# Second attention with its scores laid out by keys: TensorE alternates score chunks of the tile two ahead with value products of the present one

## The chip, the cores and the metric

One core of a Trainium2 chip runs the whole program. The metric is the device time of one execution in microseconds (us). Engines: PE is TensorE (PEld its weight loads), DVE VectorE, ACT ScalarE, POOL GpSimd, SP SyncE, which here only starts transfers. They run their own instruction lists and meet at semaphores.

## What is computed

The program runs a convolutional attention block on 4 images of 48x48 tokens with 128 channels, then full self-attention over the 2304 tokens of each image, then a routed expert layer. Only the second attention (`layer1_attention`) is touched:

```
def _L1_attn_ref(x, Wq, bq, Wk, bk, Wv, bv):
    q = x @ Wq + bq
    k = x @ Wk + bk
    v = x @ Wv + bv
    scores = jnp.einsum('btd,bsd->bts', q, k)
    attn = jax.nn.softmax(scores, axis=-1)
    return jnp.einsum('bts,bsd->btd', attn, v)

t = t + _L1_attn_ref(_ln_t(t), ...)     # t: 4 images x 2304 tokens x 128
```

Everything is float32. One attention head has 128 channels, so for each image the score matrix is 2304x2304.

## The kernel before

An image has 18 query tiles (`TILES`) of 128 tokens. Keys come in 6 chunks (`NG`) of 384, that is 3 blocks of 128 (`GB`). `lnT` holds the normalised tokens with channels on partitions; the key weights are folded into the queries, so `lnT` serves as the keys and `qT` as the queries. `v` holds the values by tokens, and in one more column a per-token constant that is added to the scores.

For each query tile the engines do this, with 128 queries on partitions:

- PE (`scores`, L1264): six products of 128x384 into `Sps`, with the query tile as the stationary weights; VectorE (`stage`, L1456) copies that tile out of `qT` first.
- DVE (`take_scores`, L1463): adds the constant, writes the chunk to `S` and keeps its row maximum; L1467 makes the negative maximum of the six.
- ACT (`tile`, L1140): one exponential over 128x2304, whose bias is that maximum, with the row's total as a by-product.
- PE (`attend`, L1287): 18 transposes of the exponentials into `Tps`, since the value product needs keys on partitions. ACT (L1148) copies them to `PT` in six pieces of 128x384.
- PE (`values`, L1278): 18 products of 128x128, with a block of `PT` as the stationary weights, added up in `Ops`.
- DVE (`take_row`, L1471 and L1477; `row_statistics`, L1483 to L1489): scales by the inverse total, adds to the token rows, and takes their mean and variance.

PE works one tile ahead with the scores. All instructions stand in hand-written order, one list for each engine. Into the tiles of images 0 to 2 the preparation of the next image is spread (`PROJECT` at tile 8, `TRANSPOSE` at 11, `TO_Q` at 12, `TO_V` at 14 on PE; sums, statistics and normalisation on DVE behind tiles 0, 1, 3, 5, 6, 8, 9 and 10). In the last image the results are normalised by POOL (`normal`, L1088) and transposed by PE ahead of tiles 5, 8 and 11 for the expert layer. POOL otherwise adds a bias to the next image (`bias`, L1075, 128x384 x6) and computes `rstd2`.

Of the kernel before, what the change touches and what calls it, by code (L numbers as in the profile page):

```python
# [20 lines left out]
P = 128  # L21
# [911 lines left out]
def layer1_attention(nc, a, s, ident, conv_bias, x1, ln2, ln2T, sums, first_num, first_in, first_den, den_in):  # L933
# [4 lines left out]
    with ExitStack() as ctx:  # L938
# [10 lines left out]
        PT = ln2T[:, 3, :].rearrange("p (t q) -> p t q", t=TILES)  # L949
# [4 lines left out]
        v = sb("v", [P, 2 * TILES, C + 1])  # L954
# [4 lines left out]
        q_tile = sb("q_tile", [P, 2, P])  # L959
        S = sb("S", [P, 2, N])  # L960
        weights = sb("weights", [P, 3, C])
# [12 lines left out]
        part_max = sb("part_max", [P, 2, NG])  # L974
        neg_max = sb("neg_max", [P, 2])
        total = sb("total", [P, 2])
# [7 lines left out]
        Sps = ps("Sps", [P, 3, BANK])  # L984
        Tps = ps("Tps", [P, 3, BANK])
# [13 lines left out]
        q_staged, s_ready, s_taken = sem("q_staged"), sem("s_ready"), sem("s_taken")  # L999
        max_ready, p_ready, inv_step, row_step = sem("max_ready"), sem("p_ready"), sem("inv_step"), sem("row_step")  # L1000
        moments_ready, rstd_step, rstd_ready, ln2_ready = sem("moments_ready"), sem("rstd_step"), sem("rstd_ready"), sem("ln2_ready")

        S_SLOTS = T_SLOTS = 3
        O_SLOTS = 2
        S_USES = NG * TILES
# [8 lines left out]
        def t_at(b, qt, last=False, after=True):  # L1014

            if last:
                return T_PREP + (T_PREP + NG * TILES) * b + NG * (qt + sum(qt >= x if after else qt > x for x in TO_EXPERTS))
            prep = sum(qt >= x if after else qt > x for x in (TRANSPOSE, TO_Q))
            return T_PREP + (T_PREP + NG * TILES) * b + NG * (qt + prep)

        def o_at(b, qt, last=False, after=True):
            prep = 0 if last else sum(qt >= x if after else qt > x for x in (PROJECT, TO_V))
            return O_PREP + (O_PREP + TILES) * b + qt + NG * prep
# [37 lines left out]
        def _(pool):  # L1061
# [41 lines left out]

        @block.scalar
        def _(act):
            for i, w in enumerate(("Wo0", "Wq1", "Wk1")):
                act.dma_start(weights[:, i, :], a[w]).then_inc(weights_in, 16)
            act.dma_start(value[:, 0:C], a["Wv1"]).then_inc(weights_in, 16)
# [7 lines left out]
            def take_transposes(n, i, groups=range(NG)):  # L1116
                for g in groups:
                    act.wait_ge(t_ready, n + g + 1)
                    act.activation(lnT[:, bass.ds((i % 2) * N + g * GW, GW)], Tps[:, g % T_SLOTS, 0:GW], ACT.Copy).then_inc(t_taken, 1)

            def take_queries(n, i):
                for g in range(NG):
                    act.wait_ge(t_ready, n + g + 1)
                    alone(act)
                    act.activation(qT[:, bass.ds((i % 2) * N + g * GW, GW)], Tps[:, g % T_SLOTS, 0:GW], ACT.Identity,
                                   bias=query[:, C:C + 1]).then_inc(t_taken, 1)

            def take_normal(b, n, groups):
                for g in groups:
                    act.wait_ge(t_ready, n + g + 1)  # L1130
                    act.activation(ln2T[:, b, cols(GW, g)], Tps[:, g % T_SLOTS, 0:GW], ACT.Copy,
                                   accum_out=sums[:, b, g:g + 1]).then_inc(t_taken, 1)

            BEFORE, BEHIND = range(T_SLOTS), range(T_SLOTS, NG)

            def tile(b, qt, t, last=False, before=None, prepare=()):
                if before is not None:
                    before()
                act.wait_ge(max_ready, TILES * b + qt + 1)
                act.activation(S[:, t, :], S[:, t, :], ACT.Exp, bias=neg_max[:, t:t + 1],  # L1140
                               accum_out=total[:, t:t + 1]).then_inc(p_ready, 1)
                for step in prepare:
                    step()
                for g in range(NG):
                    if g == 0:
                        act.wait_ge(o_ready, o_at(b, qt, last))
                    act.wait_ge(t_ready, t_at(b, qt, last) + g + 1)
                    act.activation(PT[:, cols(GB, g), :], Tps[:, g % T_SLOTS, 0:GW].rearrange("p (t q) -> p t q", t=GB),  # L1148
                                   ACT.Copy).then_inc(t_taken, 1)
# [20 lines left out]
            for b in range(B - 1):  # L1170
                prepare = {
                    TRANSPOSE - 1: [lambda: deviations(b + 1)],
# [837 lines left out]
```

## Time and profile before

| | us |
|---|---|
| median of 3 runs (lowest, highest) | 3510.87 (3508.09, 3511.03) |
| profiled execution, its own time | 3511.96 |
| its span | 3510.2 |
| tiles of the second attention, first score product to last row | 2575.4 to 3347.9 |
| expert layer's first instruction on PE | 3353.66 |

Busy over the span: PE 3403.2 us (97%), PEld 2643.6, DVE 2635.0, ACT 2015.6, POOL 1645.1. In the profile a PE instruction's time reaches to its modelled end, and neighbours overlap; the distance between starts is what the engine spends.

### The profile page before, as it was taken

The numbers are of one execution on the slowest core, as the hardware profiler recorded it, in microseconds if no ns is written. First come the engines' busy times: TensorE is split into PE (matmuls) and PEld (weight loads), VectorE is DVE, ScalarE is ACT, GpSimd is POOL, SyncE is SP. The second block draws the span as 40 slices with busy tenths as digits, with TensorE's granted clock in tenths as the row PEclk, the third lists the DMA queues.
The fourth block names the chain that finished last, engine by engine and source line by source line (L and its number), as shares of the span: only waits on it lengthen the run. The fifth ranks groups of instructions, "written<-read, shape, count | busy, mean of one in ns | idle before, by whom it ended". The sixth has DMA issues, their size and how long they took to land. (4 is left out here: it accounts for less than half of the span.)

```text
span 3510.2 us, 94134 instructions
## 1 busy us (share of the span) xinstructions
PE 3403.2 (97%) x30646; PEld 2643.6 (75%) x30646; DVE 2635.0 (75%) x6494; ACT 2015.6 (57%) x3642; POOL 1645.1 (47%) x863
## 2 busy tenths in 40 slices
PE   8799999999999999999999999999799999999978
PEld 5477777777777777777777777777578888888867
DVE  8688888888888888888888888888666675654457
ACT  4466666666666666666666666666435454455533
POOL 5566656556556556656656655655400001005112
PEclk9899999999999999999999999999899999999989
DMA  7642242234224224222422422222331020100011
GB/s 266 194 133 94 72 135 94 72 106 123 73 99 129 72 92 136 73 92 100 109 92 94 115 92 94 81 91 94 106 99 58 15 85 4 39 1 1 1 44 42
DMA packets 111794, 308.21 MB, mean 88 GB/s; under 512 B 11592, under 2 KB 72955, under 8 KB 91163
## 3 DMA queue, kind: packets, MB, share of 16 engines
q1 hardware_dynamic: 110629, 306.27, 27.9%
q8 instruction: 68, 1.11, 0.1%
q10 hardware_dynamic: 1054, 0.48, 0.1%
q14 instruction: 43, 0.35, 0.0%
HBM read 252.38 MB, written 54.31 MB: 87 GB/s over the span
## 5 line engine op out<-in xcount | busy, mean ns | idle before, releaser
L730 ACT ACTIVATE c_PT<-c_Tps 128x512 f32<-128x512 f32 x2592 | 1428.3, 604 | 877.8 <-PE c_Tps L860 815.7
L795 DVE CUSTOM_DVE_ANT_0 c_S<-c_Sps,mask_tiles 128x768 f32<-128x768 f32 x1728 | 1619.3, 956 | 412.6 <-PE c_Sps L849 371.8
L698 POOL TENSOR_SCALAR c_S<-c_S,c_row_max 128x2304 f32<-128x2304 f32 x576 | 1414.0, 2455 | 950.6 <-DVE c_row_max L806 950.6
L860 PE MATMUL c_Tps<-ident,c_S 128*128 128x128 f32 x10368 | 1400.8, 273 | 4.1 <-ACT c_PT L730 4.1
L860 PEld LDWEIGHTS c_Tps<-ident,c_S 128*128 128x128 f32 x10368 | 1229.7, 140 | 152.1 <-ACT c_PT L730 9.7
L849 PE MATMUL c_Sps<-c_K,c_Q 96*128 (+1 forms) x3456 | 854.6, 328 | 29.0 <-DVE c_part_max L795 14.6
L873 PE MATMUL c_Ops<-c_PT,c_V 128*32 128x256 f32 x10368 | 619.2, 382 | 0.8 <-ACT c_PT L730 0.8
L873 PEld LDWEIGHTS c_Ops<-c_PT,c_V 128*32 128x32 f32 x10368 | 307.4, 109 | 243.6 <-issue 51.1
L849 PEld LDWEIGHTS c_Sps<-c_K,c_Q 96*128 96x128 bf16 x3456 | 315.2, 98 | 188.4 <-issue 144.1
L1463 DVE TENSOR_SCALAR_CACHE_REDUCE l_S<-l_Sps,l_v 128x384 f32<-128x384 f32 x432 | 259.8, 618 | 252.9 <-PE l_Sps L1264 249.3
L1148 ACT ACTIVATE ln2T<-l_Tps 128x384 f32<-128x384 f32 x432 | 196.5, 491 | 363.6 <-PE l_Tps L1287 363.6
L1278 PE MATMUL l_Ops<-l_v,ln2T 128*128 128x128 f32 x2592 | 336.3, 275 | 0.1
L1278 PEld LDWEIGHTS l_Ops<-l_v,ln2T 128*128 128x128 f32 x2592 | 317.6, 192 | 19.1 <-issue 0.6
L1080 POOL TENSOR_SCALAR l_rstd<-l_moments 128x3 f32<-128x3 f32 x24 | 5.6, 235 | 681.0 <-DVE l_moments L1489 681.0
L788 DVE SCALAR_TENSOR_TENSOR c_conv<-c_vpad,taps,c_conv (+1 forms) x216 | 304.9, 1412 | 10.4 <-issue 5.6
L1264 PE MATMUL l_Sps<-l_lnT,l_q_tile 128*128 128x384 f32 x864 | 305.8, 488 | 2.2 <-issue 0.9
L1264 PEld LDWEIGHTS l_Sps<-l_lnT,l_q_tile 128*128 128x128 f32 x864 | 151.9, 190 | 85.0 <-DVE l_S L1463 13.8
L1287 PE MATMUL l_Tps<-ident,l_S 128*128 128x128 f32 x1296 | 188.9, 273 | 1.5 <-ACT l_S L1140 0.8
L1287 PEld LDWEIGHTS l_Tps<-ident,l_S 128*128 128x128 f32 x1296 | 152.8, 141 | 25.4 <-issue 12.2
L1140 ACT ACTIVATE l_S<-l_S,l_neg_max 128x2304 f32<-128x2304 f32 x72 | 159.0, 2208 | 8.6 <-DVE l_neg_max L1467 8.6
L795 DVE DVE_READ_ACCUMULATOR2_ANT c_part_max<- 128x1 f32 x1728 | 143.5, 83 | 0.0
L1693 ACT ACTIVATE e_hid<-e_Hps,e_b 128x384 f32<-128x384 f32 x96 | 55.7, 582 | 65.2 <-PE e_Hps L1728 62.2
(223 smaller groups left out, 1644.2 us busy)
## 6 DMA issues: line engine op xcount, KB each, us to landing
mask_tiles<-in_mask SPq DMA_DIRECT2D x144, 1152.0 KB, 7.7
numerators<-c_O SPq DMA_DIRECT2D x288, 64.0 KB
mask_tiles<-numerators SPq DMA_DIRECT2D x7, 2304.0 KB, 8.5
q_parts<-c_PT SPq DMA_DIRECT2D x12, 576.0 KB, 4.4
k_parts<-c_PT SPq DMA_DIRECT2D x12, 576.0 KB
c_Q<-q_parts SPq DMA_DIRECT2D x71, 96.0 KB
c_vpad<-v_padded SPq DMA_DIRECT2D x8, 756.0 KB, 14.8
c_K<-k_parts SPq DMA_DIRECT2D x7, 864.0 KB, 8.6
```

The costliest lines, as they stand in the source:

```text
L698: pool.tensor_scalar(S[:, slot, :], S[:, slot, :], -1.0, row_max[:, slot:slot + 1], ALU.mult, ALU.add).then_inc(shifted, 1)
L730: act.activation(dst, src, ACT.Exp, scale=-1.0).then_inc(exp_done, 1)
L788: dve.scalar_tensor_tensor(out=dst, in0=window[:, :, 0:W], scalar=taps[:, bass.ds(tap, 1)], in1=dst, op0=ALU.mult, op1=ALU.add).then_inc(c ...
L795: dve.tensor_tensor_reduce(out=S[:, r % ROW_SLOTS, cols(CH, c)].rearrange("p (k n) -> p k n", k=2), in0=Sps[:, n % S_SLOTS, :, 0:GW], in1= ...
L849: last = pe.matmul(Sps[:, n % S_SLOTS, k, 0:GW], Q[:, p, r // 2, cols(P, r % 2)], K[:, bass.ds(start, GW)], start=True, stop=True)
L860: last = pe.transpose(Tps[:, g % T_SLOTS, cols(P, k)], S[:, (2 * b + t) % ROW_SLOTS, cols(P, kt)], ident[:, :])
L873: last = pe.matmul(Ops[32 * j:32 * (j + 1), image, :], V[:, b * TILES + kt, :], PT[:, image, kt, :], start=kt < COLS, stop=kt >= TILES - COLS)
L1148: act.activation(PT[:, cols(GB, g), :], Tps[:, g % T_SLOTS, 0:GW].rearrange("p (t q) -> p t q", t=GB), ACT.Copy).then_inc(t_taken, 1)
L1264: pe.matmul(Sps[:, g % S_SLOTS, 0:GW], q_tile[:, t, :], lnT[:, bass.ds((b % 2) * N + g * GW, GW)], start=True, stop=True).then_inc(s_ready, 1)
L1278: product = pe.matmul(Ops[:, t, 0:C], PT[:, kt, :], v[:, (b % 2) * TILES + kt, 0:C], start=kt == 0, stop=kt == TILES - 1)
L1287: block_t = pe.transpose(Tps[:, g % T_SLOTS, cols(P, k)], S[:, t, cols(P, g * GB + k)], ident[:, :])
L1463: dve.tensor_scalar(S[:, t, cols(GW, g)], Sps[:, g % S_SLOTS, 0:GW], v[:, (b % 2) * TILES + qt, C:C + 1], None, ALU.add, ALU.max, accum_ou ...
```

## The change

Scores are computed with keys on partitions: `lnT`'s block of 128 keys is the stationary operand and the query tile (read straight from `qT`, so `stage` is gone) streams through it, 18 products of 128x128 in six chunks. The exponentials then stand as the value product needs them, and the 18 transposes of a tile and their copies go. What goes with them:

- ACT copies each score chunk from `Tps` (now four slots) to one of three buffers `keys_by` (`take_scores`).
- The maximum of a query now lies across partitions and blocks. DVE reduces the nine blocks of each half (`half_maximum`: 128x1152 in, 128x128 out, read with the block index innermost, so each element lies 128 words behind the last), joins the halves (`key_maximum`), PE turns that 128x128 tile (`turn_max`), DVE reduces it to one number per query and writes it into a 128x128 tile together with the constant (`query_maximum`), PE turns that back (`spread_max`), and ACT copies it to `shift` (`take_shift`).
- `shift` is subtracted from all 18 blocks: the first nine by DVE, the last nine by POOL (`subtract_max`, 128x1152 each). ACT then takes the exponential of each half (`exponentials`).
- `v` gets a column of ones, so the value product of 129 columns also gives the total; `take_row` inverts it.
- PE alternates: chunk g of tile j+2, then the three value products g of tile j, six times; `turn_max(j+1)` stands after g=1 and `spread_max(j+1)` after g=2.
- POOL's bias, deviations and normalisations are spread over the tiles behind its subtraction.

The core of the diff (functions rewritten in full are shown as after):

```diff
-        Sps = ps("Sps", [P, 3, BANK])
-        Tps = ps("Tps", [P, 3, BANK])
+        Tps = ps("Tps", [P, 4, BANK])
+        Mps = ps("Mps", [P, 2, BANK])
+        P_SLOTS = 3
+        keys_by = [slot.rearrange("p (t q) -> p t q", t=TILES) for slot in (S[:, 0, :], S[:, 1, :], ln2T[:, 3, :])]
...
@@ gpsimd
+            def subtract_max(j):
+                pool.wait_ge(shift_in, j + 1)
+                part = keys_by[j % P_SLOTS][:, HALVES[1].start:HALVES[1].stop, :]
+                pool.tensor_tensor(part, part, shift[:, :, :].to_broadcast([P, len(HALVES[1]), P]), ALU.subtract).then_inc(shifted_pool, 1)
...
@@ scalar
+            for j in range(1, ALL):
...
+                if j + AHEAD < ALL:
+                    take_scores(j + AHEAD, range(TURN + 2))
+                if j + 1 < ALL:
+                    take_shift(j + 1)
+                if j + AHEAD < ALL:
+                    take_scores(j + AHEAD, range(TURN + 2, NG - 1))
+                if j + 1 < ALL:
+                    exponentials(j + 1, 0)
+                if j + AHEAD < ALL:
+                    take_scores(j + AHEAD, range(NG - 1, NG))
+                if j + 1 < ALL:
+                    exponentials(j + 1, 1)
...
@@ tensor
+                for g in range(NG):
+                    if j + AHEAD < ALL:
+                        scores(j + AHEAD, range(g, g + 1))
+                    values(j, g)
+                    if j + 1 < ALL and g == TURN:
+                        turn_max(j + 1)
+                    if j + 1 < ALL and g == TURN + 1:
+                        spread_max(j + 1)
...
@@ vector
+            def half_maximum(j, half):
+                dve.wait_ge(t_taken, scores_at(j) + NG * (half + 1) // 2 + T_SLOTS)
+                part = keys_by[j % P_SLOTS][:, HALVES[half].start:HALVES[half].stop, :].rearrange("p t q -> p q t")
+                dve.tensor_reduce(half_max[:, half, :], part, AX.X, ALU.max).then_inc(half_step, 1)
...
+            def query_maximum(j):
+                dve.wait_ge(turned_max, j + 1)
+                dve.tensor_reduce(query_max[:, :], Mps[:, 0, 0:P], AX.X, ALU.max).then_inc(query_step, 1)
...
+                dve.scalar_tensor_tensor(out=max_wide[:, :], in0=query_max[:, :].to_broadcast([P, P]), scalar=constant,
+                                         in1=constant.to_broadcast([P, P]), op0=ALU.add, op1=ALU.subtract).then_inc(wide_max, 1)
...
+            def subtract_max(j):
+                dve.wait_ge(shift_in, j + 1)
...
+            for j in range(ALL):
+                if j:
+                    take_row(j - 1)
...
+                if j:
+                    row_statistics(j - 1)
+                if j and j + 1 < ALL:
+                    query_maximum(j + 1)
+                if j + AHEAD < ALL:
+                    half_maximum(j + AHEAD, 0)
+                if j + 1 < ALL:
+                    subtract_max(j + 1)
+                if j + AHEAD < ALL:
+                    half_maximum(j + AHEAD, 1)
+                    key_maximum(j + AHEAD)
```

How it moves instructions. On PE, one tile in the middle of an image, before (x is the number of products; the 6 score products stand as 5 and 1):

```order
L1264 MATMUL l_Sps<-l_lnT,l_q_tile 128x384 x5
L1287 MATMUL l_Tps<-ident,l_S 128x128 x9
L1264 MATMUL l_Sps<-l_lnT,l_q_tile 128x384
L1278 MATMUL l_Ops<-l_v,ln2T 128x128 x3
L1287 MATMUL l_Tps<-ident,l_S 128x128 x3
L1278 MATMUL l_Ops<-l_v,ln2T 128x128 x3
L1287 MATMUL l_Tps<-ident,l_S 128x128 x3
L1278 MATMUL l_Ops<-l_v,ln2T 128x128 x3
L1287 MATMUL l_Tps<-ident,l_S 128x128 x3
L1278 MATMUL l_Ops<-l_v,ln2T 128x128 x9
```

and the first three and a half of the six rounds of such a tile after:

```order
L1310 MATMUL l_Tps<-l_qT,l_lnT 128x128 x3
L1330 MATMUL l_Ops<-l_v,l_S 128x129 x3
L1310 MATMUL l_Tps<-l_qT,l_lnT 128x128 x3
L1330 MATMUL l_Ops<-l_v,l_S 128x129 x3
L1316 MATMUL l_Mps<-ident,l_key_max 128x128
L1310 MATMUL l_Tps<-l_qT,l_lnT 128x128 x3
L1330 MATMUL l_Ops<-l_v,l_S 128x129 x3
L1322 MATMUL l_Mps<-ident,l_max_wide 128x128
L1310 MATMUL l_Tps<-l_qT,l_lnT 128x128 x3
```

The transposes of whole score tiles have left PE, and two single ones that carry the maximum stand between the rounds.

On DVE, the same place before:

```order
L1463 TENSOR_SCALAR l_S,l_part_max<-l_Sps,l_v 128x384 x6
L1467 TENSOR_REDUCE l_neg_max<-l_part_max 128x1
L1456 COPY l_q_tile<-l_qT 128x128
L1471 RECIPROCAL l_inv_total<-l_total 128x1
L1477 SCALAR_TENSOR_TENSOR x<-l_Ops,l_inv_total,x 128x128
L1483 BN_STATS l_row_stats<-x 128x6
L1486 BN_AGGR l_row_moments<-l_row_stats 128x2
L1489 COPY l_moments<-l_row_moments 128x2
```

and after:

```order
L1527 RECIPROCAL l_inv_total<-l_Ops 128x1
L1529 SCALAR_TENSOR_TENSOR x<-l_Ops,l_inv_total,x 128x128
L1536 BN_STATS l_row_stats<-x 128x6
L1539 BN_AGGR l_row_moments<-l_row_stats 128x2
L1542 COPY l_moments<-l_row_moments 128x2
L1509 TENSOR_REDUCE l_query_max<-l_Mps 128x1
L1516 SCALAR_TENSOR_TENSOR l_max_wide<-l_query_max,l_v 128x128
L1500 TENSOR_REDUCE l_half_max<-l_S 128x128
L1522 TENSOR_TENSOR l_S<-l_S,l_shift 128x1152
L1500 TENSOR_REDUCE l_half_max<-l_S 128x128
L1504 TENSOR_TENSOR l_key_max<-l_half_max 128x128
```

The six reads of PSUM have become two reductions and a subtraction over half a tile each, and four of the eleven rows now belong to tiles one or two ahead.

## Rows read from the trace of the kernel before

**Rows 1.** Page, part 5: busy us, mean ns | idle before, TensorE and ScalarE groups of this stage.

```profile
L1278 PE MATMUL l_Ops<-l_v,ln2T 128*128 128x128 f32 x2592 | 336.3, 275 | 0.1
...
L1264 PE MATMUL l_Sps<-l_lnT,l_q_tile 128*128 128x384 f32 x864 | 305.8, 488 | 2.2 <-issue 0.9
...
L1287 PE MATMUL l_Tps<-ident,l_S 128*128 128x128 f32 x1296 | 188.9, 273 | 1.5 <-ACT l_S L1140 0.8
...
L1148 ACT ACTIVATE ln2T<-l_Tps 128x384 f32<-128x384 f32 x432 | 196.5, 491 | 363.6 <-PE l_Tps L1287 363.6
```

**Rows 2.** Windows: length, busy PE, PEld, DVE, ACT, POOL, granted clock, DMA share, GB/s.

```profile
2619.45:2814.51 195.06, 194.44 (x1291) 160.31 (x1290) 121.13 (x423) 97.49 (x160) 12.48 (x18) 1.00 0.14 45
...
2764.34:2774.19 9.85, 9.85 (x68) 8.21 (x67) 4.94 (x19) 4.92 (x9) 0.00 (x0) 1.00 0.00 0
...
2555.00:2565.00 10.00, 6.08 (x20) 3.85 (x21) 6.44 (x30) 3.26 (x7) 0.00 (x0) 0.63 1.03 398
```

**Rows 3.** Timeline, TensorE, one tile: start us, us, engine, line.

```profile
2762.43 2.17 PE L1278 MATMUL l_Ops<-l_v,ln2T 128*128 128x128 f32 x18
...
2764.44 3.39 PE L1264 MATMUL l_Sps<-l_lnT,l_q_tile 128*128 128x384 f32 x10
...
2767.67 1.15 PE L1287 MATMUL l_Tps<-ident,l_S 128*128 128x128 f32 x9
...
2774.30 0.49 PE L1264 MATMUL l_Sps<-l_lnT,l_q_tile 128*128 128x384 f32 x1
```

**Rows 4.** Timeline, VectorE, the same tile and the next.

```profile
2765.39 0.62 DVE L1463 TENSOR_SCALAR_CACHE_REDUCE l_S<-l_Sps,l_v 128x384 f32<-128x384 f32 x1 [3.50 <-PE l_Sps L1264]
...
2770.37 0.16 DVE L1471 RECIPROCAL l_inv_total<-l_total 128x1 f32<-128x1 f32 x1
...
2770.45 0.33 DVE L1477 SCALAR_TENSOR_TENSOR x<-l_Ops,l_inv_total,x 128x128 f32<-128x128 f32 x1
...
2774.56 0.35 DVE L1477 SCALAR_TENSOR_TENSOR x<-l_Ops,l_inv_total,x 128x128 f32<-128x128 f32 x1 [2.82 <-PE l_Ops L1278]
...
2775.82 0.62 DVE L1463 TENSOR_SCALAR_CACHE_REDUCE l_S<-l_Sps,l_v 128x384 f32<-128x384 f32 x1
```

**Rows 5.** Groups by form over the whole run, VectorE: busy us, mean ns.

```profile
L1354 DVE TENSOR_TENSOR mask_tiles<-mask_tiles 128x1152 f32<-128x1152 f32 x12 | 15.6, 1344 | 0.0
...
L1841 DVE TENSOR_TENSOR mask_tiles<-mask_tiles,e_b2s 128x2304 f32<-128x2304 f32 x4 | 10.2, 2551 | 0.0
...
L1796 DVE TENSOR_REDUCE e_r<-e_greater 4x8 f32<-4x128 f32 x1 | 0.3, 274 | 0.0
...
L1506 DVE COPY l_bo_all<-l_Tps 128x128 f32<-128x128 f32 x3 | 0.7, 281 | 0.0
...
L1870 DVE SCALAR_TENSOR_TENSOR mask_tiles<-mask_tiles,e_ymv,e_gamma 128x128 f32<-128x128 f32 x72 | 20.6, 341 | 0.0
...
L1347 DVE TENSOR_TENSOR l_den_sum<-first_den 128x144 f32<-128x144 f32 x4 | 1.2, 307 | 0.1
```

**Rows 6.** Groups by form over the whole run, GpSimd.

```profile
L271 POOL TENSOR_TENSOR f_rot_sum<-f_rot_sum,c_PT 128x768 f32<-128x768 f32 x23 | 38.2, 1659 | 42.0 <-ACT c_PT L315 41.9
...
L1075 POOL TENSOR_TENSOR ln2T<-ln2T,l_bo_all 128x384 f32<-128x384 f32 x24 | 23.2, 1000 | 28.1 <-DMA ln2T<-in_x 28.1
```

**Rows 7.** Timeline, GpSimd and VectorE at 2777 us, and VectorE at 2525 us.

```profile
2777.10 5.84 POOL L1075 TENSOR_TENSOR ln2T<-ln2T,l_bo_all 128x384 f32<-128x384 f32 x6
...
2781.05 2.07 DVE L1344 TENSOR_TENSOR first_den<-first_den 128x144 f32<-128x144 f32 x2
...
2525.49 0.53 DVE L1344 TENSOR_TENSOR first_den<-first_den 128x144 f32<-128x144 f32 x2 [0.57 <-DMA first_den<-denominators]
```

**Rows 8.** Groups by form, ScalarE.

```profile
L1140 ACT ACTIVATE l_S<-l_S,l_neg_max 128x2304 f32<-128x2304 f32 x72 | 159.0, 2208 | 8.6 <-DVE l_neg_max L1467 8.6
...
L1160 ACT ACTIVATE l_query<-l_Ops 128x129 f32<-128x129 f32 x1 | 0.3, 280 | 2.0 <-PE l_Ops L1207 2.0
```

**Rows 9.** Timeline, ScalarE, inside the tile of rows 3.

```profile
2768.26 1.26 ACT L1148 ACTIVATE ln2T<-l_Tps 128x384 f32<-128x384 f32 x3 [2.94 <-PE l_Tps L1287]
```

More of the change, by code:

```diff
@@ L1130, in take_normal @@
                     act.wait_ge(t_ready, n + g + 1)
-                    act.activation(ln2T[:, b, cols(GW, g)], Tps[:, g % T_SLOTS, 0:GW], ACT.Copy,
+                    act.activation(ln2T[:, b, cols(GW, g)], Tps[:, (n + g) % T_SLOTS, 0:GW], ACT.Copy,
                                    accum_out=sums[:, b, g:g + 1]).then_inc(t_taken, 1)
[L1134 to L1149, printed above, removed]
@@ L1180, in normal_part @@
[L1180 to L1187 removed]
+            take_scores(0, range(NG))
+            take_scores(1, range(NG))
@@ new lines, in _ @@
+            take_shift(0)
+            take_scores(2, range(4))
+            exponentials(0, 0)
+            take_scores(2, range(4, NG))
+            exponentials(0, 1)
+            take_shift(1)
+            for half in range(2):
+                exponentials(1, half)
+            for j in range(1, ALL):
+                b, qt = j // TILES, j % TILES
+                if b == B - 1:
+                    if qt in TO_EXPERTS:
+                        take_normal(TO_EXPERTS.index(qt), t_at(j))
+                elif qt == TRANSPOSE:
+                    take_transposes(t_at(j), b + 1)
+                elif qt == TO_Q:
+                    take_queries(t_at(j), b + 1)
+                if j + AHEAD < ALL:
[10 more added lines that the diff above has]
+                    exponentials(j + 1, 1)
+                if b + 1 < B and qt == TRANSPOSE - 1:
+                    deviations(b + 1)
@@ L1324, in _ @@
-            for qt in range(TILES):
-                if qt in TO_EXPERTS:
-                    transpose_normal(TO_EXPERTS.index(qt), t_at(B - 1, qt, last=True, after=False))
-                following = (B - 1, qt + 1, (qt + 1) % 2) if qt + 1 < TILES else None
-                if following is not None:
-                    scores(*following, groups=FIRST)
-                attend(B - 1, qt, qt % 2, last=True, last_scores=following)
+            scores(0, range(NG))
+            scores(1, range(3))
@@ new lines, in _ @@
+            turn_max(0)
+            scores(1, range(3, NG))
+            spread_max(0)
+            scores(2, range(4))
+            turn_max(1)
+            scores(2, range(4, NG))
+            pe.wait_ge(o_taken, O_PREP + O_SLOTS)
+            for g in range(NG):
+                values(0, g)
+                if g == 2:
+                    spread_max(1)
+            for j in range(1, ALL):
+                b, qt = j // TILES, j % TILES
+                if b == B - 1:
+                    if qt in TO_EXPERTS:
+                        transpose_normal(TO_EXPERTS.index(qt), t_at(j))
+                elif qt == PROJECT:
+                    project(b + 1, o_at(j, after=False))
+                elif qt == TRANSPOSE:
+                    transpose_ln(b + 1, t_at(j))
+                elif qt == TO_Q:
+                    to_q(b + 1, t_at(j))
+                elif qt == TO_V:
+                    to_v(b + 1, o_at(j, after=False))
+                for g in range(NG):
+                    if j + AHEAD < ALL:
[5 more added lines that the diff above has]
+                        spread_max(j + 1)
```

373 lines of the change are left out of this document (167 added, 206 removed).

## The prediction

> **What bounds the kernel now.** I read the page's groups of the stage first, then windows, then one tile on each engine. The stage takes 772.5 us of the span (the tiles run from 2575.4 to 3347.9). In a window that spans one whole image TensorE is busy for 194.44 of 195.06 us, and in one of a single plain tile for 9.85 of 9.85, at full clock, while VectorE and ScalarE are busy for about half of it [rows 2]. So a tile costs what TensorE needs, and the timeline takes that apart [rows 3]. 18 instructions of value products last 2.17 us together and one of them 0.275 [rows 1], so they start (2.17 - 0.275)/17 = 0.1115 us apart; each float32 product is two instructions, so 0.223 us. Transposes: (1.15 - 0.273)/8 = 0.110. Score instructions of 384 columns: (3.39 - 0.488)/9 = 0.322. A tile is 12 x 0.322 + 18 x 0.110 + 36 x 0.1115 = 3.87 + 1.98 + 4.01 = 9.86 us, and its starts are 2774.30 - 2764.44 = 9.86 apart. VectorE waits for TensorE at the tile's head (3.50 us idle [rows 4]).
>
> **What the change does to TensorE.** 18 score products of 128 columns with new weights each are what the value products already are: 0.223 each, 4.01 us, against 3.87. The transposes go (-1.98), two single ones come (+0.22), and one column more in 36 instructions adds 36 x 0.1115/128 = 0.03. TensorE's tile is 3.87 -> 4.01, in sum 8.28 us, 1.58 less. If TensorE stayed the bound, 72 tiles would give back 114 us.
>
> **What it does to the others.** I follow the order of each list around one tile, since VectorE now stands between every two steps. A hop from one engine to another I take as 0.1 us: the third transpose of rows 3 ends at 2767.67 + 2 x 0.110 + 0.273 = 2768.16, and ScalarE's copy starts at 2768.26 [rows 9]. Starting from the moment at which `query_maximum` can run:
>
> 1. `query_maximum`: a reduction of 128 numbers from PSUM, 0.28 (the 4x128 reduction took 0.274, a PSUM copy of 128 0.281 [rows 5]), 0.1 for the own semaphore, and a 128x128 SCALAR_TENSOR_TENSOR, 0.34 [rows 5]: 0.72.
> 2. hop, `spread_max` 0.28, hop, `take_shift` 0.28 (128x129 from PSUM [rows 8]), hop: 0.86. Meanwhile VectorE does `half_maximum(j+2, 0)`, so it is not waiting when `shift` arrives, and POOL is.
> 3. POOL's subtraction over 128x1152. 384 elements took 1.000 and 768 took 1.659 us [rows 6]; another 384 make 1.659 + 0.659 = 2.32.
> 4. VectorE's subtraction, also with both operands in SBUF. Such an instruction does not run beside POOL's: two 128x144 ones took 0.53 us alone and 2.07 while POOL worked through its six of 128x384, which start 0.97 apart [rows 7], so each waited for one POOL instruction to end. I take it that it starts after POOL's: 1.3 (1152 elements are 1.344 alone [rows 5]).
> 5. hop, then ScalarE's `exponentials(j+1, 0)`. From 129 to 384 columns a ScalarE instruction grows by 0.211 us [rows 1, 8], 0.83 ns a column; 2304 take 2.208, so 1152 take 2.208 - 0.953 = 1.25. Only behind it stands the copy of the sixth score chunk, 0.385 (three take 1.26, the last 0.49 [rows 9]). Hop. In all 1.84, in which VectorE has nothing, because its next instruction needs that chunk.
> 6. `half_maximum(j+2, 1)`, h, then `key_maximum`, 0.33 with its own semaphore (0.307 for 144 elements [rows 5]).
> 7. `take_row` and `row_statistics` of the finished tile. From the reciprocal to the scaling 0.08, from the scaling to the first instruction behind the statistics 1.26 [rows 4]: 1.34. Then step 1 again.
>
> The circle is 0.72 + 0.86 + 2.32 + 1.3 + 1.84 + h + 0.33 + 1.34 = 8.71 + h. `turn_max` is in time in a plain tile: TensorE starts the next tile's values 1.35 us after step 4 ends, needs 0.67 + 1.34 us to reach it, and VectorE gets there after 1.84 + h + 0.33.
>
> h is a reduction over 1152 elements each 512 bytes from the last, and no row has such a read. Contiguous, 128 elements take 0.274 and 1152 of another instruction 1.344; were each element to cost two, it would be the 2.551 of 2304 elements [rows 5]. Between 1.34 and 2.55 neither end is nearer in kind; I take the middle, 1.95. The circle is 10.66, rounded to 10.6 for what the 0.1 hops overstate: 0.75 more than 9.85.
>
> The Trainium skill (Vector Engine (DVE) Microarchitecture Reference, section 5.2, on the access granule) has a table for element orders: 1.054 ns a column contiguous, 1.73 when a source hops on every element, and 2.50 at a step of 24 words. That would be an estimate of 1152 x 1.73 + 80 = 2.07 us, or 2.96, and the circle by it 10.7 or 11.6. The trace here can't show it.
>
> **Preparation.** It was hidden under TensorE and is no longer. VectorE is busy 121.13 us in an image's window and 4.94 in a plain tile [rows 2], so 121.13 - 18 x 4.94 = 32.2 us an image are preparation. 12 instructions of 0.56 of it (PSUM to `x` and to `v`, 6.7 us) run against TensorE's 18 products of 0.223. Those two tiles then need another round and a half before `turn_max`: 4.0 + 2.7 - 1.3 is about 5.5 each instead. The other 25.5 us stand in series in the circle. At `TRANSPOSE` and `TO_Q` ScalarE's six copies begin only behind both exponentials, and `turn_max` comes about 2.3 us late, twice. Together 25.5 + 11 + 4.6 = 41 us an image. Before, an image took 195.06 - 18 x 9.85 = 17.8 us above its tiles. So three images get 18 x 0.75 + 23 = 36.7 us longer, 110; the last one 13.5 and 1 for the transposes of the expert layer; the first tile starts its values later, but no scores are left at the end: 0. In all +124 us. The profiled execution took 3511.96, 1.1 above the median of the runs: 3511.96 + 124 = 3636.
>
> **Rivals.**
> - *The read costs nothing extra.* h = 1.34, 0.61 less in 72 circles: -44, so 3592. For it: VectorE's rows are all alike per element. Against: all of them read neighbours.
> - *The read costs two elements or more.* h = 2.55: +43, 3679. The page named above has a step at which it is dearer still, and its 2.96 as an estimate would give 3709.
> - *Faster: the two subtractions run side by side.* If VectorE's does not wait for POOL's, it starts when `half_maximum(j+2, 0)` ends, and the circle is 0.72 + h + 1.34 + 1.84 + h + 0.33 + 1.34 = 5.57 + 2h. With h = 1.34 that is 8.25, and TensorE's 8.28 decide: 1.57 less a tile, -113, against 3 x 20 for preparation (23 less a little that VectorE's spare time takes up) and 1: about 3460. It ends below the kernel before only up to a circle of 8.9 (72 x 0.95 are those 69), h about 1.65; with h = 1.95 (9.47) it gives 3554. For it: only one place in the stage shows POOL in VectorE's way, and in 128x144. Against: that place is clear, 2.07 against 0.53.
> - *The clock.* TensorE waits 2.3 of 10.6 us. At 61% busy the granted clock was 0.63 [rows 2], a mixture of its two levels (1.2 and 2.4 GHz). At the lower one a tile would be 16.6 us and the time about 4000. It would stay busy then, so at worst this comes in pieces; it decides only where a stretch falls below a clock of 8.28/10.6 = 0.78.
>
> **How the numbers follow.** Forecast case (POOL first, h from 1.6 to 2.3, 3611 to 3662): 0.58. Costlier read: 0.15. Free read with the wait for POOL: 0.10. Side by side with a costly read: 0.05. Side by side with a free one, faster: 0.08. Clock: 0.04. A price of POOL of 3 x 0.97 instead of 2.32 adds 43 us, and hops of 0.05 take off 14. The range, 3570 to 3720, leaves out the faster case, the side-by-side ones and the clock. Runs of the kernel before differ by 0.08%; within 0.2% (7 us) I call the same. Faster 0.08, same 0.02, slower 0.90.
>
> **What would show it.** TensorE's tile without waits at 8.3 us but starts 10.6 apart, with idle time before `spread_max`, `turn_max` and a tile's first value product; L1500 at 1.95 us; VectorE's L1522 long, from the end of L1500 to 1.3 us behind POOL's L1096, which takes 2.3; 1.8 us of idle VectorE before each second L1500; an image 232 us long. Wrong would be L1522 at 1.34 beside a running L1096, or TensorE without waits.

## The result, and the profile after

| | before | after |
|---|---|---|
| median, us (lowest, highest) | 3509.70 (3508.09, 3511.03), 4 runs | 3667.28 (3666.41, 3670.36), 4 runs |
| profiled execution, span | 3511.96, 3510.2 | 3667.56, 3665.8 |
| mean granted clock over the span | 0.985 | 0.971 |
| expert layer's first instruction on PE | 3353.69 | 3510.37 |

The ratio is 1.045, 95% interval 1.0436 to 1.0464: 157 us slower. All of it arises in this stage, since the expert layer starts 156.7 us later. (The 3353.66 of the table before the prediction is the start of that instruction's weight load.) The groups of the stage, of TensorE, VectorE, GpSimd and ScalarE, in place of those of [rows 1] (busy us, mean ns | idle before):

```profile
L1310 PE MATMUL l_Tps<-l_qT,l_lnT 128*128 128x128 f32 x2592 | 375.5, 284 | 0.0
...
L1096 POOL TENSOR_TENSOR l_S<-l_S,l_shift 128x1152 f32<-128x1152 f32 x48 | 128.8, 2683 | 443.1 <-ACT l_shift L1170 443.1
...
L1330 PE MATMUL l_Ops<-l_v,l_S 128*128 128x129 f32 x1728 | 254.5, 286 | 31.4 <-ACT l_S L1175 31.4
L1500 DVE TENSOR_REDUCE l_half_max<-l_S 128x128 f32<-128x1152 f32 x96 | 208.2, 2169 | 82.6 <-ACT l_S L1165 82.6
...
L1175 ACT ACTIVATE l_S<-l_S 128x1152 f32<-128x1152 f32 x96 | 111.2, 1158 | 65.8 <-DVE l_S L1522 64.3
```

TensorE's value products now stand idle before them (31.4 us, for the exponentials), where L1278 had 0.1 [rows 1]. Windows of one image, of one plain tile, and of two stretches in the tile of `TO_V`, to be read beside [rows 2] (length, busy PE, PEld, DVE, ACT, POOL, granted clock, DMA share, GB/s):

```profile
2820.46:3062.94 242.48, 190.02 (x1436) 178.38 (x1435) 187.56 (x281) 103.10 (x178) 70.76 (x36) 0.92 0.11 37
2809.72:2820.46 10.74, 8.95 (x76) 8.41 (x75) 8.72 (x12) 5.16 (x10) 4.82 (x3) 1.00 0.00 2
2779.00:2784.00 5.00, 5.00 (x24) 5.00 (x25) 1.95 (x4) 0.00 (x0) 0.00 (x0) 0.50 0.00 0
2784.00:2789.00 5.00, 5.00 (x45) 5.00 (x45) 2.32 (x7) 1.43 (x3) 0.00 (x0) 0.97 0.01 3
```

The roles are exchanged. An image takes 242.48 us instead of 195.06, and a plain tile 10.74 instead of 9.85. TensorE was busy for all of that tile and is for 8.95 us of it now (its modelled ends included), at full clock; VectorE went from 4.94 to 8.72, and of the 2.02 us left 1.61 are one wait. One turn of the circle in the timeline of VectorE, with GpSimd's and ScalarE's parts under it (start us, us, engine, line, [idle before it <- what ended that]):

```profile
2765.15 2.18 DVE L1500 TENSOR_REDUCE l_half_max<-ln2T 128x128 f32<-128x1152 f32 x1 [1.61 <-ACT ln2T L1165]
2767.37 0.29 DVE L1504 TENSOR_TENSOR l_key_max<-l_half_max 128x128 f32<-128x128 f32 x1
2767.58 0.16 DVE L1527 RECIPROCAL l_inv_total<-l_Ops 128x1 f32<-128x1 f32 x1
...
2768.98 0.28 DVE L1509 TENSOR_REDUCE l_query_max<-l_Mps 128x1 f32<-128x128 f32 x1
2769.30 0.35 DVE L1516 SCALAR_TENSOR_TENSOR l_max_wide<-l_query_max,l_v 128x128 f32<-128x128 f32 x1
2769.57 2.17 DVE L1500 TENSOR_REDUCE l_half_max<-l_S 128x128 f32<-128x1152 f32 x1
2771.67 2.62 DVE L1522 TENSOR_TENSOR ln2T<-ln2T,l_shift 128x1152 f32<-128x1152 f32 x1
2775.89 2.11 DVE L1500 TENSOR_REDUCE l_half_max<-l_S 128x128 f32<-128x1152 f32 x1 [1.61 <-ACT l_S L1165]
...
2770.43 2.64 POOL L1096 TENSOR_TENSOR ln2T<-ln2T,l_shift 128x1152 f32<-128x1152 f32 x1 [8.10 <-ACT l_shift L1170]
...
2774.32 1.16 ACT L1175 ACTIVATE ln2T<-ln2T 128x1152 f32<-128x1152 f32 x1 [1.74 <-DVE ln2T L1522]
2775.39 0.47 ACT L1165 ACTIVATE l_S<-l_Tps 128x384 f32<-128x384 f32 x1
2775.76 1.15 ACT L1175 ACTIVATE ln2T<-ln2T 128x1152 f32<-128x1152 f32 x1
```

From the second half's reduction to the next such one it is 2775.89 - 2765.15 = 10.74 us. VectorE's subtraction (L1522) is on record as 2.62 us, because it starts at 2771.67 beside GpSimd's, which ends at 2773.07, and ends 1.22 behind it. Then VectorE stands idle for 1.61 us, until ScalarE has done an exponential half and, behind it, the copy of the sixth score chunk. Every step of the circle is in these rows.

### The profile page after: what moved, and what is told of

It reads as the page before. It is cut to its first block and busy times, and to the rows that moved or that the text cites. A ratio compares the mean times of both kernels' runs of the same rounds, so it can differ in the third digit from the quotient of the medians.

```text
span 3665.8 us, 94647 instructions
## 1 busy us (share of the span) xinstructions
PE 3367.5 (92%) x31222; PEld 2699.3 (74%) x31222; DVE 2903.7 (79%) x5918; ACT 2035.4 (56%) x3714; POOL 1881.2 (51%) x936
## 5 line engine op out<-in xcount | busy, mean ns | idle before, releaser
L1310 PE MATMUL l_Tps<-l_qT,l_lnT 128*128 128x128 f32 x2592 | 375.5, 284 | 0.0
L1096 POOL TENSOR_TENSOR l_S<-l_S,l_shift 128x1152 f32<-128x1152 f32 x48 | 128.8, 2683 | 443.1 <-ACT l_shift L1170 443.1
L1310 PEld LDWEIGHTS l_Tps<-l_qT,l_lnT 128*128 128x128 f32 x2592 | 347.3, 203 | 1.1
L1330 PE MATMUL l_Ops<-l_v,l_S 128*128 128x129 f32 x1728 | 254.5, 286 | 31.4 <-ACT l_S L1175 31.4
L1500 DVE TENSOR_REDUCE l_half_max<-l_S 128x128 f32<-128x1152 f32 x96 | 208.2, 2169 | 82.6 <-ACT l_S L1165 82.6
L1165 ACT ACTIVATE l_S<-l_Tps 128x384 f32<-128x384 f32 x288 | 138.9, 487 | 210.8 <-PE l_Tps L1310 210.7
L1330 PEld LDWEIGHTS l_Ops<-l_v,l_S 128*128 128x128 f32 x1728 | 228.0, 201 | 37.0 <-issue 37.0
L1096 POOL TENSOR_TENSOR ln2T<-ln2T,l_shift 128x1152 f32<-128x1152 f32 x24 | 64.4, 2683 | 183.0 <-ACT l_shift L1170 183.0
L1175 ACT ACTIVATE l_S<-l_S 128x1152 f32<-128x1152 f32 x96 | 111.2, 1158 | 65.8 <-DVE l_S L1522 64.3
L1500 DVE TENSOR_REDUCE l_half_max<-ln2T 128x128 f32<-128x1152 f32 x48 | 104.5, 2177 | 38.8 <-ACT ln2T L1165 38.8
L1330 PE MATMUL l_Ops<-l_v,ln2T 128*128 128x129 f32 x864 | 122.9, 280 | 5.6 <-ACT ln2T L1175 5.5
```

The costliest lines, as they stand in the source:

```text
L1096: pool.tensor_tensor(part, part, shift[:, :, :].to_broadcast([P, len(HALVES[1]), P]), ALU.subtract).then_inc(shifted_pool, 1)
L1165: act.activation(keys_by[j % P_SLOTS][:, cols(GB, g), :], Tps[:, (scores_at(j) + g) % T_SLOTS, 0:GW].rearrange("p (t q) -> p t q", t=GB), ...
L1310: last = pe.matmul(Tps[:, (n + g) % T_SLOTS, cols(P, k)], lnT[:, bass.ds((b % 2) * N + (g * GB + k) * P, P)], query_tile, start=True, stop ...
L1330: last = pe.matmul(Ops[:, qt % 2, 0:C + 1], keys_by[j % P_SLOTS][:, kt, :], v[:, (b % 2) * TILES + kt, 1:C + 2], start=kt == 0, stop=kt == ...
L1500: dve.tensor_reduce(half_max[:, half, :], part, AX.X, ALU.max).then_inc(half_step, 1)
```

## The experiments

Two edits act on links of the circle (e2, e3), one on the reduction (e1), and one on where the preparation stands (e4). The others put these together and follow what then decides. "Plain tile" is a tile without preparation, as the distance between the starts of `query_maximum`; "image" is the third one, between the same starts (the second differs from it by up to 1.7 us); "preparation" is an image less 18 plain tiles. The row "before" has the second image, between first score products. Each ratio is against executions of the kernel before from the same round, whose medians lie between 3509.1 and 3509.7.

| kernel | time, us (lowest, highest) | ratio, 95% interval | plain tile | image | preparation |
|---|---|---|---|---|---|
| before | 3509.70 | 1 | 9.85 | 195.06 | 17.8 |
| after | 3667.28 | 1.045 (1.0436 to 1.0464) | 10.74 | 242.4 | 49.1 |
| e1 contiguous reductions | 3615.10 (3614.10, 3617.04) | 1.0303 (1.0286 to 1.0320) | 9.90 | 229.0 | 50.8 |
| e2 sixth copy first | 3573.47 (3572.69, 3577.66) | 1.0187 (1.0170 to 1.0204) | 9.40 | 218.4 | 49.2 |
| e3 shift from PSUM | 3589.01 (3588.28, 3590.64) | 1.0228 (1.0211 to 1.0245) | 9.46 | 225.3 | 55.0 |
| e4 preparation in the gap | 3649.77 (3648.93, 3652.17) | 1.0403 (1.0386 to 1.0420) | 10.74 | 235.2 | 41.9 |
| e5 = e2 + e3 | 3557.46 (3554.25, 3558.36) | 1.0134 (1.0118 to 1.0149) | 8.88 | 215.1 | 55.3 |
| e6 = e5 + e4 | 3525.02 (3523.41, 3527.34) | 1.0043 (1.0027 to 1.0058) | 8.88 | 204.6 | 44.8 |
| e7 = e5 + contiguous | 3513.64 (3511.32, 3517.26) | 1.0012 (1.0002 to 1.0021) | 8.88 | 201.4 | 41.6 |
| e8 = e5 + sums on GpSimd | 3534.54 (3533.45, 3535.24) | 1.0072 (1.0058 to 1.0085) | 8.88 | 208.2 | 48.4 |
| e9 = e5 + scores earlier | 3505.94 (3504.91, 3510.80) | 0.9994 (0.9985 to 1.0003) | 8.38 | 201.4 | 50.6 |
| e10 = e6 + sums + scores earlier | 3489.24 (3484.12, 3490.05) | 0.9939 (0.9925 to 0.9952) | 8.37 | 194.8 | 44.1 |
| e11 = e7 + scores earlier | 3471.07 (3469.69, 3472.84) | 0.9889 (0.9874 to 0.9904) | 8.26 | 191.2 | 42.5 |

**e1: what the reduction's read costs.** In `half_maximum`:

```diff
-                part = keys_by[...][:, HALVES[half].start:HALVES[half].stop, :].rearrange("p t q -> p q t")
+                part = keys_by[...][:, HALVES[half].start:HALVES[half].stop, :].rearrange("p t q -> p (t q)").rearrange("p (q t) -> p q t", t=TILES // 2)
```

> The two reductions of a half tile read the same 1152 numbers in the order in which they lie, so what they give is no maximum per query; all else as in the changed kernel (3667). My theory: the circle through VectorE sets each tile (10.74 us), the second reduction of each tile lies on it and the first is hidden behind GpSimd's subtraction. The reduction goes from 2.17 to 1.34 us, the circle to 9.9, the time falls by 72 x 0.83 = 60 to about 3607. Rival A, TensorE is what lasts (its granted clock fell to 0.9 in this stage and its products lie further apart): the reductions are beside the point and the time falls by under 10. Rival B, both reductions lie in series: 120 less.

The groups of VectorE:

```profile
L1522 DVE TENSOR_TENSOR l_S<-l_S,l_shift 128x1152 f32<-128x1152 f32 x48 | 157.1, 3273 | 4.2 <-ACT l_shift L1170 4.2
L1500 DVE TENSOR_REDUCE l_half_max<-l_S 128x128 f32<-128x1152 f32 x96 | 129.7, 1351 | 84.2 <-ACT l_S L1165 84.0
```

The same 1152 elements take 1.351 us when neighbours are read, and 2.169 when each lies 512 bytes from the last. Both reductions of a tile got 0.82 shorter, but the tile only by 0.84 in all: the first one ended sooner into the wait for GpSimd, and L1522 grew from 2500 to 3273 ns. So one reduction of the two lies on the circle, as the prediction had it. The run gained 52 us of the 60 expected, since preparation grew by 1.7 us an image. A cheap read alone doesn't make the change pay.

**e2: the idle stretch.** In ScalarE's list:

```diff
-                    take_scores(j + AHEAD, range(TURN + 2, NG - 1))
+                    take_scores(j + AHEAD, range(TURN + 2, NG))
                 if j + 1 < ALL:
                     exponentials(j + 1, 0)
-                if j + AHEAD < ALL:
-                    take_scores(j + AHEAD, range(NG - 1, NG))
-                if j + 1 < ALL:
                     exponentials(j + 1, 1)
```

> ScalarE copies the sixth score chunk ahead of the first exponential, not behind it. My theory: VectorE's 1.61 us of idle time before each second reduction goes, the circle becomes 9.1 to 9.2 (the other circle, through exponential, first value products and turn_max, is 9.0 and lies just below), 110 us less: about 3557. Rival: the exponential comes later, TensorE's first value products wait for it in its place, and the circle through TensorE keeps the time within 20 us of 3667.

```profile
L1497 DVE TENSOR_REDUCE l_half_max<-l_S 128x128 f32<-128x1152 f32 x96 | 208.2, 2170 | 26.5 <-ACT l_S L1165 26.5
```

L1497 is `half_maximum` in this kernel. The idle time ahead of it falls from 82.6 to 26.5 us, the tile by 1.34, and the run by 94 us: of the three costs that were cut one by one (e1 to e3) the largest is the order of two ScalarE instructions. The tile came 0.2 to 0.3 us longer than expected.

**e3: the shared access of VectorE and GpSimd.** VectorE's subtraction reads the shift where TensorE left it, in PSUM, instead of the SBUF copy; GpSimd keeps the copy. `spread_max` then waits for that subtraction instead of the copy.

```diff
-                    pe.wait_ge(shift_in, j)
+                    pe.wait_ge(shifted_dve, j)
...
-                dve.tensor_tensor(part, part, shift[:, :, :].to_broadcast([P, len(HALVES[0]), P]), ALU.subtract)
+                dve.tensor_tensor(part, part, Mps[:, 1:2, 0:P].to_broadcast([P, len(HALVES[0]), P]), ALU.subtract)
```

> VectorE's subtraction reads the shift from PSUM and not from its SBUF copy, so only one of its operands lies in SBUF; it still waits for the copy. My theory: it need no longer wait for GpSimd's subtraction, lasts 1.36 us right behind the first reduction, the circle loses 1.25 us, 90 less: about 3577, and GpSimd's subtraction stays at 2.64. Rival: the instruction lasts 2.6 us for another reason (in place, broadcast operand) and the time does not move; or from PSUM it is slower by itself.

VectorE and GpSimd in a plain tile, where GpSimd's subtraction starts first:

```profile
3207.07 1.34 DVE L1522 TENSOR_TENSOR ln2T<-ln2T,l_Mps 128x1152 f32<-128x1152 f32 x1
...
3205.84 2.64 POOL L1096 TENSOR_TENSOR ln2T<-ln2T,l_shift 128x1152 f32<-128x1152 f32 x1 [7.09 <-ACT l_shift L1170]
```

Side by side and each at its own price, in all 72 tiles (1.335 to 1.359 us and 2.632 to 2.659). The wait was for what two SBUF operands need and not for the data, which are the same. The tile loses 1.28 us, the run 78 and not 90, since preparation grew from 49.1 to 55.0 us an image.

**e4: preparation into the idle stretch.** The steps that stood behind `key_maximum` (`invert`, `sum_half` and so on) stand ahead of it and of the second half's reduction:

```diff
                     subtract_max(j + 1)
+                if b + 1 < B:
+                    if qt == 0:
+                        invert(b + 1)
...
                 if j + AHEAD < ALL:
                     half_maximum(j + AHEAD, 1)
                     key_maximum(j + AHEAD)
```

> The eight pieces of preparation on VectorE stand between its subtraction and the second reduction, where it idles 1.61 us, not behind the reduction. My theory: preparation is in series in the circle, and here each piece hides up to 1.6 us of itself: seven of 1.6 and one of 1.2 in three images, 37 less, some of it lost to GpSimd's bias: 3630 to 3640. Rival: preparation costs by its transfers, TensorE and ScalarE parts, and the time stays within 8 us of 3667.

7.2 us an image came back, of at most 8 x 1.6 = 13 that the idle stretches of the eight tiles with such steps hold. The run gained 17.5 us: between the theory (27 to 37) and the rival (under 8). In the second image the tiles of seven of the steps got 1.0 to 1.8 us shorter, but the tile of `PROJECT` 1.0 longer, and that of `normalise` and `TRANSPOSE` stayed at 19 us. Some steps grew there beside GpSimd's subtraction: `sum_half`'s L1399 took up to 2.04 us, 1.59 on average, instead of 1.36.

**e5: both links.**

> The two edits of the second and third experiment together: the sixth copy ahead of the middle value products, and VectorE's subtraction reading the shift from PSUM. My theory (a circle of 18 x waits between VectorE and GpSimd sets a tile's period): the two act on different links, 1.34 us (10.74 to 9.40) and 1.28 us (10.74 to 9.46) off the circle, so a tile that does nothing else takes 8.1 to 8.4 us, where TensorE's own 8.28 us begins to matter; with the preparation as before the time is 3667 - 94 - 78 = 3495, and less of a gain where TensorE's 8.28 takes over, 3500 to 3515. A rival, that one of the two gains came through the same wait as the other (the idle time ahead of the exponentials), would leave the circle at 9.3 to 9.4 and the time near 3570.

Neither. 8.88 is neither 8.1 to 8.4 nor 9.3, and the run fell 62 us short of the sum of the two gains (3495). Something new decides at 8.88.

**e6, e7, e8: what decides then.**

> The fifth experiment with the preparation steps ahead of the second half's reduction, as in the fourth. If the fourth experiment gained (18 us) because the steps filled VectorE's idle stretch ahead of that reduction, there is next to nothing left to fill once that stretch is gone, and this one ends within 10 us of the fifth. If it gained because the steps in that place stretch less beside GpSimd or reach TensorE sooner, it is again 15 to 20 us under the fifth.

> The fifth experiment with the second half's reduction over neighbouring elements, of the same size: its maximum is no longer the one of each query, so the outputs differ. VectorE's part of a tile falls by another 0.8 us (2.17 to 1.35). If the fifth is held by TensorE's instructions (8.28 us in a tile that does nothing else), such a tile stays at 8.28 to 8.35, and only the tiles with preparation gain, some 5 to 10 x 0.8 us an image, so 12 to 25 us in all. If VectorE's circle still sets the period there, every tile gains up to 0.8 us, some 40 us in all.

> The fifth experiment with the additions of the partial sums, 3.9 us of VectorE in each of two tiles of an image, done by GpSimd in the tiles 1, 2, 5 and 6, where it has 3 to 4 us free beside its two steps. If VectorE's work in those tiles adds to the period as it did in the changed kernel (tiles 3.9 us longer), the time falls by 3 x 2 x 3.9 = 23 us against the fifth, to some 3480 to 3490. If GpSimd's additions (near 2 us each) come in the way of its subtraction, or stretch VectorE beside them, the gain is under 8 us.

In e7 both halves' reductions read neighbours (the expectation names only the second), so VectorE has 0.8 us less to do in each half, and the plain tile stays at 8.88 to the hundredth. The run gained 44 us all the same, near the 40 of the theory that failed, but nearly all of it in preparation (55.3 to 41.6 us an image). So VectorE isn't what holds it there, and 8.88 isn't TensorE's 8.28 either. TensorE's timeline of e7, its first value products in two tiles that follow each other, gives the reason:

```profile
3197.05 0.91 PE L1327 MATMUL l_Ops<-l_v,l_S 128*128 128x129 f32 x6 [0.38 <-ACT l_S L1175]
...
3205.93 0.91 PE L1327 MATMUL l_Ops<-l_v,ln2T 128*128 128x129 f32 x6 [0.38 <-ACT ln2T L1175]
```

TensorE waits in every tile for the first exponential half. The idle time is reckoned from modelled ends; by starts, the score chunk ahead and these value products take 1.96 us together instead of 1.34, and 0.62 on top of the 8.26 that e11 shows is 8.88. By e2's edit that half stands behind the sixth copy, and the copy behind the last score chunk, which TensorE computes only one group of value products before. It is e2's gain on one engine turned into a wait on another, hidden as long as VectorE was later still.

e6 was meant as a control and fell outside both theories: 32 us under e5, where 0 or 15 to 20 were expected. An image lost 10 to 11 us, most of it in two tiles: 3.9 in the one behind `statistics` (12.85 to 8.96 in the second image) and 2.7 in that of the second `finish_half`. The rows of the first are TensorE's. First e5's, in the timeline and in windows:

```profile
2915.23 0.48 PE L1319 MATMUL l_Mps<-ident,l_max_wide 128*128 128x128 f32 x1 [3.19 <-DVE l_max_wide L1513]
2915.50 1.49 PE L1307 MATMUL l_Tps<-l_qT,l_lnT 128*128 128x128 f32 x6
```

```profile
2916.00:2921.00 5.00, 5.00 (x25) 5.00 (x25) 2.50 (x2) 1.00 (x3) 2.64 (x1) 0.50 0.00 0
2921.00:2926.00 5.00, 4.62 (x40) 4.46 (x39) 3.63 (x21) 3.46 (x5) 0.00 (x0) 0.98 0.00 0
```

Then e6's, the same two views:

```profile
2896.15 0.34 PE L1313 MATMUL l_Mps<-ident,l_key_max 128*128 128x128 f32 x1 [1.80 <-DVE l_key_max L1501]
2896.32 0.83 PE L1307 MATMUL l_Tps<-l_qT,l_lnT 128*128 128x128 f32 x6
```

```profile
2895.00:2900.00 5.00, 3.53 (x30) 3.34 (x31) 4.58 (x10) 1.26 (x3) 1.13 (x1) 1.00 0.00 0
```

In e5 the step (`statistics`, 3.57 us) stands between `key_maximum` and the next `query_maximum`, and TensorE stands for 3.19 us before `spread_max`. Then its clock is granted at 0.50, which is 1.2 GHz: in the next 5 us six instructions (three products) take 1.29 us instead of 0.67. In e6 the same step delays `turn_max` instead, TensorE stands for 1.80 us, and the clock stays at 1.00. From 2820 to 3020 us the mean clock is 0.93 in e5 and 0.97 in e6, and TensorE's idle time before `spread_max` 16.2 and 1.7 us (before `turn_max` in e6 8.0). So the placing is worth more than the idle stretch it fills, and part of it may be the clock. How much of the 32 us is clock and how much the shorter wait wasn't tried by itself.

e8 moves the additions to GpSimd:

```diff
+            def sum_pairs(i, half):
+                pool.wait_ge(half_in, 16 * (2 * i + half - 1))
+                for x in (0, 2):
+                    last = pool.tensor_tensor(num[:, x, :], num[:, x, :], num[:, x + 1, :], ALU.add)
+                last.then_inc(sum_step, 1)
...
+                if b + 1 < B and qt in (1, 2):
+                    (sum_pairs if qt == 1 else sum_sums)(b + 1, 0)
+                if b + 1 < B and qt in (5, 6):
+                    (sum_pairs if qt == 5 else sum_sums)(b + 1, 1)
```

The time fell by 23 us, as expected (from 3557 that is 3534; the 3480 to 3490 of the expectation doesn't follow from its own sum), but otherwise than expected: an addition takes GpSimd 2.65 us, where I had put 2, and because the second `finish_half` went one tile later, the tile of `PROJECT` took 20.2 us instead of 16.7.

**e9: the new wait.** In TensorE's list the sixth score chunk goes ahead of the fifth group of value products:

```diff
                 for g in range(NG):
-                    if j + AHEAD < ALL:
-                        scores(j + AHEAD, range(g, g + 1))
+                    if j + AHEAD < ALL and g < NG - 1:
+                        scores(j + AHEAD, range(g, NG if g == NG - 2 else g + 1))
                     values(j, g)
```

> The fifth experiment, with the sixth score chunk of the tile two ahead computed before the fifth group of value products instead of after it. In the fifth and the seventh experiment alike a plain tile took 8.88 us, in each TensorE stood 0.4 to 0.5 us before its first value products (for ScalarE's first exponential half, which stands behind the sixth copy). My theory now: 8.28 us of instructions and this wait make the 8.88. Then the sixth copy comes 0.67 us sooner, the wait goes, and a plain tile takes 8.3 to 8.5 us (VectorE's own circle with the strided reduction is near 8.45): 0.4 us x some 45 tiles, 3535 to 3542 us. If instead VectorE's circle holds the 8.88 (the seventh showed that it doesn't alone), the time stays at 3557.

The group of value products of e5, and then of e9:

```profile
L1327 PE MATMUL l_Ops<-l_v,l_S 128*128 128x129 f32 x1728 | 252.6, 285 | 17.5 <-ACT l_S L1175 17.5
```

```profile
L1327 PE MATMUL l_Ops<-l_v,l_S 128*128 128x129 f32 x1728 | 239.5, 280 | 0.9 <-ACT l_S L1175 0.9
```

The wait is gone and the plain tile is 8.38, in the expected range. The run gained 51 us, more than twice the 15 to 22 expected: all 72 tiles got 0.5 us shorter and not some 45 (36 us), and the preparation 4.7 us an image (14), which I hadn't counted. This kernel can't be told from the one before.

**e10 and e11.**

> The sixth experiment (both edits, preparation ahead of the second half's reduction), with the edit of the ninth, and with the additions of the partial sums done by GpSimd (the first half's in the tiles 1 and 2, the second's in 4 and 5, so that the steps that use them stay where they are in the sixth). By the parts: 3525 - 17 for the wait - 19 for the additions (tiles of 11.6, 9.9 and 12.7 us in the sixth, of 11.4, 9.1 and 10.3 in the eighth) = 3489, between 3480 and 3500, which is under the kernel before (3509). If GpSimd's additions come in the way of its subtraction as they did in the tile after the eighth's sixth, 3500 to 3510.

> The seventh experiment (second half's maxima not taken per query) with the edit of the ninth: VectorE now has 0.8 us a tile to spare. A plain tile is TensorE's instructions alone, 8.28 to 8.32 us, if the theory of the ninth holds, and the image's preparation is what is left; the time falls by 0.5 us x 50 tiles under the seventh, 3487 to 3492. With a second wait of TensorE behind the first, it stays above 8.4 us a tile.

e10 takes e8's additions in other tiles: the pairs of the second half in the tiles 4 and 5, so that `finish_half` stays in tile 6. It takes 3489.24 us, as the sum of its parts had it: 0.61% under the kernel before (0.48 to 0.75). e11 gives TensorE's own price: 8.26 us for a plain tile. It came 16 us lower than expected because all 72 tiles lost 0.62 us, and not 50 of them 0.5. Its maxima aren't per query, so it is no kernel to use; against e9 it says what a reduction at neighbours' price would be worth: 35 us.

## Why the prediction was right

The direction and the place were right: 3667 us lies in the range, 31 above the 3636 forecast (157 us slower, 124 forecast). The mechanism was the forecast one, a circle through VectorE, GpSimd and ScalarE that is longer than TensorE's tile.

**TensorE.** 8.28 us a tile were worked out; e11 shows 8.26 with nothing in the way.

**The circle**, 10.6 forecast, 10.74 measured. From the rows of the tile shown, in the order of the prediction's steps (forecast in brackets): `query_maximum` 0.67 (0.72); hops, spread and copy 0.78 (0.86); GpSimd 2.64 (2.32); VectorE behind it 1.22 (1.3); to the next reduction 1.60 (1.84); h, to the start of L1504, 2.22 (1.95); `key_maximum` 0.21 (0.33); rows and statistics 1.40 (1.34). Their sum is 10.74. GpSimd and h were each some 0.3 too cheap, and the hops, the idle stretch and `key_maximum` were together 0.57 too dear. That the circle came so near is in part luck. GpSimd's 768 elements took 1.659 us [rows 6] and 1152 take 2.64, so the step from 384 to 768 wasn't one to carry on; three times the price of 384, which stood among the bounds as 2.9, was nearer.

**h.** The middle of the two bounds, 1.95, became 2.17. The Trainium skill (Vector Engine (DVE) Microarchitecture Reference, section 5.2) has 1.73 ns a column when one source hops 4 KiB on every element, an estimate of 2.07 us here, and 2.50 ns a column at steps of 24 words. The trace agrees with the first to 5%, and e1 with its contiguous price (1.351 us, by the page an estimate of 1.29). So a step of 128 words cost about what the long hops do there.

**The rivals.** "The read costs nothing extra" was to give 3592. e1 takes that cost away and gives 3615, since GpSimd's 2.64 remain. "Side by side" is excluded by L1522 in the changed kernel, and e3 makes it true: 1.35 beside a running L1096, with a plain tile of 9.46. The rival's 5.57 + 2h gives 9.9 with the h measured; the idle stretch, `key_maximum` and `query_maximum` were rated 0.4 too long in it. The Trainium skill (SBUF — State Buffer, "SBUF: two separate sides") says that of a VectorE instruction with two SBUF inputs and a GpSimd instruction that reads SBUF the one that starts first has the shared port pair for all its time, and the other waits. By the same page's "Who interferes with whom", a VectorE instruction with at most one SBUF input, outside the two-port modes, stays out of it. The trace and e3 agree with both, and in the other order too. In the last tile VectorE came first, and GpSimd's row is the long one:

```profile
3497.36 1.36 DVE L1522 TENSOR_TENSOR ln2T<-ln2T,l_shift 128x1152 f32<-128x1152 f32 x1 [0.73 <-ACT l_shift L1170]
...
3497.41 3.80 POOL L1096 TENSOR_TENSOR ln2T<-ln2T,l_shift 128x1152 f32<-128x1152 f32 x1 [8.07 <-ACT l_shift L1170]
```

**Preparation** is the term that was mis-sized: 41 us an image forecast, 49.1 measured. With the 2.5 us of the circle (18 x 0.14) that makes 10.6 us an image and 32 of the missing 33. The series part was near (`sum_half` adds 3.9 us to its tile). `TO_Q` was to add 2.3 and adds 5.2, `TO_V` 5.5 and adds 8.0.

At `TO_V` the reason is for the most part the clock. TensorE in that tile of the first image, in the changed kernel and then in e9:

```profile
2778.85 6.21 PE L1297 MATMUL l_Ops<-l_value,l_lnT 128*128 128x129 f32 x30 [4.12 <-DVE x L1529]
```

```profile
2746.21 4.25 PE L1294 MATMUL l_Ops<-l_value,l_lnT 128*128 128x129 f32 x30 [1.58 <-DVE x L1526]
```

In the changed kernel it had stood for 4.12 us, and at a granted clock of 0.50 these instructions start 0.21 us apart. In e9 the clock is 1.00 and the 30 take 1.96 us less; there, in e3 and in e7, each at a clock of 1.00, `TO_V` adds 5.7 to 6.3 us to its tile, near the forecast. At `TO_Q` it isn't the clock: in e5 this step runs at 1.00 and still adds 4.8. The forecast counted only how late its copies start, and not its 12 products and the two rounds behind them.

The rival on the clock was asked whether a plain tile falls to the lower level. It doesn't: plain tiles show a clock of 1.00, and one with a stretch at the lower level inside (0.84 in the mean) still takes 10.74, because TensorE has room there. What the prediction missed is that the clock can fall behind the waits that preparation makes, at the very place where TensorE's speed counts. The length of the wait doesn't settle it: at `TO_V` the clock fell about a wait of 2.23 us in e5 (0.68 in the mean over the 5.3 us behind it), and stayed at 1.00 about one of 2.84 in e3. What decides there stays open.

The last image was to get 14.5 us longer and got 12.2, between its first and last scaled row (L1477 before, L1529 after).

**A second circle** mattered to the experiments only: ScalarE's sixth copy, the exponential half and TensorE's first value products, at 8.88. It comes with e2's order of ScalarE's instructions and decides once the first circle is shorter.

## What to carry to other kernels

When a change relieves the engine that is the bound, write down the longest closed chain through the others, with every order and shared port in it, before counting what is saved: here TensorE was freed of 1.6 us a tile and the tile grew by 0.9. Such a chain can be cheap to cut (the order of two ScalarE instructions gave 94 us, an operand read from PSUM 78), but behind it stands the next one, so gains found one by one don't add up; look after each for the engine that has begun to wait. Work that was hidden under the old bound costs its price in the new one, and more where it makes TensorE stand and its clock falls.

## What the runs showed of the hardware

- A reduction over 128x1152 with 512 bytes from element to element took 2.17 us, over neighbours 1.35.
- GpSimd's 128x1152 TENSOR_TENSOR took 2.64 us, against 1.00 for 384 and 1.66 for 768 elements [rows 6]; VectorE's took 1.34.
- With both operands in SBUF, VectorE's TENSOR_TENSOR ended 1.22 us behind GpSimd's; with one in PSUM it took 1.35 us beside it, and GpSimd's kept its 2.65. Where VectorE's started first, it took 1.36 us and GpSimd's 3.80.
- After waits of 3.19 and 4.12 us TensorE's granted clock was 0.50 in the next 5 us window, with instructions of float32 products 0.21 us apart; after one of 1.80 us it was 1.00. A wait of 2.23 us (e5) was followed by 0.68 over 5.3 us, one of 2.84 us (e3) by 1.00.
